# First unit's queries fetched and split inside the query stage of a cross-attention kernel, normalised rows spread over three pairs, last stores waited for later

## The reference, cut to what matters

```python
def _L0_xattn_ref(x, context, Wq, Wkv, Wo, ln_g, ln_b):   # x (16,64,256), context (16,1601,256)
    ctx = _layernorm(context, ln_g, ln_b)
    q = x @ Wq                                             # 16 heads of 64
    k, v = jnp.split(ctx @ Wkv, 2, axis=-1)
    ...
    sim = jnp.einsum('bhid,bhjd->bhij', q, k) * scale
    attn = jax.nn.softmax(sim, axis=-1)
    out = jnp.einsum('bhij,bhjd->bhid', attn, v)
    ...
x = x + _L0_xattn_ref(_layernorm(x), ctx_1024, ...)
```

## Time and profile before

| what | value |
|---|---|
| runs | 1813.75, 1817.82, 1817.73 us (median 1817.73) |
| profiled execution, its own time | 1818.62 us |
| its span in the trace | 1816.9 us |
| mean granted TensorE clock | 0.966 |
| PE busy | 1691.2 us, 93% of the span |
| DVE busy | 1469.1 us, 81% |
| ACT busy | 1233.8 us, 68% |

### The profile page before, as it was taken

How to read it: one execution, slowest core, us unless ns; L and a number is a source line. 1 busy time by engine, 2 the same in 40 slices (tenths; PEclk the granted TensorE clock), 3 DMA queues, 4 the chain that set the end, 5 groups by cost and what they waited for, 6 DMA issues and landing times. The chain is left out here.

```text
span 1816.9 us, 31835 instructions
## 1 busy us (share of the span) xinstructions
PE 1691.2 (93%) x9258; PEld 1391.5 (77%) x9258; DVE 1469.1 (81%) x2927; ACT 1233.8 (68%) x2224; POOL 129.7 (7%) x122
## 2 busy tenths in 40 slices
PE   6699999999999999999999999998889559999994
PEld 4478888888888888888888888886355349999994
DVE  5689999899989998999989998886346558788763
ACT  4567778778777777787777877866225247777751
POOL 0000000000000000000000000000012230000003
PEclk9899999999999999999999999999889779999996
DMA  7732222222313222222122222002850076666632
GB/s 268 284 89 60 85 78 69 72 78 62 88 56 89 68 78 69 79 64 88 55 86 69 82 70 84 26 24 71 275 183 27 26 243 221 194 230 216 197 103 75
DMA packets 172562, 199.01 MB, mean 110 GB/s; under 512 B 19129, under 2 KB 131921, under 8 KB 172497
## 3 DMA queue, kind: packets, MB, share of 16 engines
q1 hardware_dynamic: 170960, 194.00, 33.8%
q0 software_dynamic: 1536, 4.20, 0.7%
HBM read 153.53 MB, written 44.63 MB: 109 GB/s over the span
## 5 line engine op out<-in xcount | busy, mean ns | idle before, releaser
L757 ACT ACTIVATE s<-score,rnow 128x512 f32<-128x512 f32 (+1 forms) x416 | 286.4, 689 | 254.0 <-PE score L143 249.5
L141 PE MATMUL score<-qsh,tl 128*128 128x512 f32 (+1 forms) x832 | 331.3, 398 | 17.5 <-DVE qsl L816 15.2
L142 PE MATMUL score<-qsl,th 128*128 128x512 f32 (+1 forms) x832 | 325.6, 391 | 0.0
L141 PE MATMUL acc<-ph,cl 128*128 128x512 f32 (+1 forms) x832 | 324.8, 390 | 0.8 <-DVE pl L795 0.7
L143 PE MATMUL score<-qsh,th 128*128 128x512 f32 (+1 forms) x832 | 325.4, 391 | 0.0
L142 PE MATMUL acc<-pl,ch 128*128 128x512 f32 (+1 forms) x832 | 324.4, 390 | 0.0
L143 PE MATMUL acc<-ph,ch 128*128 128x512 f32 (+1 forms) x832 | 324.4, 390 | 0.0
L789 DVE TENSOR_TENSOR s<-s,misc 128x512 f32<-128x512 f32 (+1 forms) x416 | 281.7, 677 | 9.1 <-PE misc L720 7.6
L795 DVE TENSOR_TENSOR pl<-s,ph 128x512 fp32r<-128x512 f32 (+1 forms) x416 | 283.7, 682 | 1.6 <-ACT ph L738 1.6
L738 ACT ACTIVATE ph<-s 128x512 fp32r<-128x512 f32 (+1 forms) x416 | 258.9, 622 | 2.2 <-PE acc L143 1.7
L743 ACT ACTIVATE s<-s 128x512 f32<-128x512 f32 (+1 forms) x416 | 258.3, 621 | 2.1 <-DVE s L789 2.1
(11 more groups left out here) (249 smaller groups left out, 2768.1 us busy)
## 6 DMA issues: line engine op xcount, KB each, us to landing
raw<-in_ctx_in SPq DMA_DIRECT2D x192, 128.0 KB, 2.3
turned<-in_turned_in SPq DMA_DIRECT2D x48, 512.0 KB, 3.7
wr<-in_W SPq DMA_DIRECT2D x45, 512.0 KB
queries_scratch<-stage SPq DMA_DIRECT2D x32, 512.0 KB, 3.8
qr<-queries_scratch SPq DMA_DIRECT2D x64, 256.0 KB, 3.6
outputs_scratch<-o SPq DMA_DIRECT2D x64, 256.0 KB, 2.9
at<-outputs_scratch SPq DMA_DIRECT2D x16, 1024.0 KB, 7.5
wr<-in_Wg SPq DMA_DIRECT2D x15, 1024.0 KB
```

Source lines behind the costliest of these rows:

```text
L141: pe.matmul(out, wl, mh, start=first, stop=False, **more)
L142: pe.matmul(out, wh, ml, start=False, stop=False, **more)
L757: act.activation(s[0:n, u, t, :], score[0:n, slot(0, u, t) % 2, :], ACT.Copy, scale=rnow[0:n, t:t + 1]).then_inc(copied, 1)
```

## The change

Four edits. First, the raw and split buffers of the queries, their semaphores, and the semaphores of the stores move into an object `Queries` that lives through both stages; the first unit's load is issued in `queries` behind the stores of pair 4, and its splits stand in pair 5. Second, the 13 normalised rows are spread over pairs 5, 6 and 7. Third, the end of `queries` on SyncE waits for the stores of pairs 2 and 5 only (semaphore `stored[2]`); all stores are waited for before the load of the second unit (SyncE) and before the first copy of the second unit's scores (ScalarE). Fourth, GpSimd sets the columns first and clears afterwards.

```diff
+ROWS_BEHIND = {(5, 1): (0, 3), (6, 0): (3, 6), (6, 1): (6, 9), (7, 0): (9, 11), (7, 1): (11, KT)}
...
+class Queries:
+    def __init__(self, sb, sem):
+        self.raw = sb("qr", [P, DC, UQ], F32)
+        self.high = sb("qsh", [P, 2, DC, UQ], F32R)
+        self.low = sb("qsl", [P, 2, DC, UQ], F32R)
+        self.arrived, self.high_made, self.low_made = sem("q_in"), sem("qs_high"), sem("qs_low")
+        self.stored = [sem(f"stored{n}") for n in range(STAGES)]
+    def load(self, sp, QT, r, u):
+        for c in range(DC):
+            src = QT[u * PAIRS // 2:(u + 1) * PAIRS // 2, :, c, bass.ds(r, 1), :]
+            sp.dma_start(self.raw[:, c, :]..., src...).then_inc(self.arrived, 16)
+    def split_high(self, v, u, loads):
+        v.wait_ge(self.arrived, 16 * DC * loads)
+        v.tensor_copy(self.high[:, u], self.raw[:, :, :]).then_inc(self.high_made, 1)
+    def split_low(self, v, u, loads):
+        v.wait_ge(self.high_made, loads)
+        v.tensor_tensor(self.low[:, u], self.raw[:, :, :], self.high[:, u].bitcast(F32), ALU.subtract
+                        ).then_inc(self.low_made, 1)
... queries, SyncE
+                    if p == PAIRS // 2:
+                        for n, s in enumerate(stored):
+                            sp.wait_ge(s, 64 * len(range(n, PAIRS // 2, STAGES)))
+                        first.load(sp, QT, 0, 0)
                 sp.wait_ge(gb_in, 32)
-                for n, s in enumerate(stored):
-                    sp.wait_ge(s, 16 * 4 * len(range(n, PAIRS, STAGES)))
+                sp.wait_ge(stored[2], 64 * len(range(2, PAIRS, STAGES)))
... queries, VectorE, behind each take
+                        if (p, th) == (5, 0):
+                            first.split_high(v, 0, 1)
+                        if (p, th) == (5, 1):
+                            first.split_low(v, 0, 1)
+                            v.wait_ge(c_shift, 1)
+                        if (p, th) in ROWS_BEHIND:
+                            rows_normalised(*ROWS_BEHIND[p, th])
...
-                    if p >= 6:
-                        v.wait_ge(c_shift, 1)
-                        for t in range(7 * (p - 6), min(7 * (p - 5), KT)):
-                            ...
... attend, SyncE
-                    if (f := k.unit(-9)):
+                    if fetched(f := k.unit(-9)):
                         r, u = f
-                        wait(sp, q_low, unit(r, u))
-                        for c in range(DC):
-                            ...
+                        if begins(r) and u == 1:
+                            for i, landed in enumerate(stored):
+                                sp.wait_ge(landed, 64 * len(range(i, PAIRS, STAGES)))
+                        sp.wait_ge(q_low, unit(r, u))
+                        first.load(sp, QT, r, u)
... attend, GpSimd
-                clear(pool, earlier)
                 pool.memset(ch[:, :, 0:1].bitcast(F32), 1.0).then_inc(counting, 1)
                 pool.memset(cl[:, :, 0:1].bitcast(F32), 0.0).then_inc(counting, 1)
+                clear(pool, earlier)
... attend, ScalarE, before the copy of the scores
+                        if begins(r) and u == 1 and t == 0:
+                            for i, landed in enumerate(stored):
+                                act.wait_ge(landed, 64 * len(range(i, PAIRS, STAGES)))
... attend, VectorE: both splits now `if fetched(...)`, that is, not for the first unit
```

More of the change, by code:

```diff
@@ L224, in pool_root @@
         pool.tensor_tensor(self.shift[:, :], self.negmu[:, :], self.rstd[:, :], ALU.mult).then_inc(c_shift, 1)
+class Queries:
[8 more added lines that the diff above has]
+            src = QT[u * PAIRS // 2:(u + 1) * PAIRS // 2, :, c, bass.ds(r, 1), :]
+            sp.dma_start(self.raw[:, c, :].rearrange("p (k n) -> p k n", n=2 * NQ),
+                         src.rearrange("k p a n -> p k (a n)")).then_inc(self.arrived, 16)
+    def split_high(self, v, u, loads):
[5 more added lines that the diff above has]
+                        ).then_inc(self.low_made, 1)
 def queries(nc, res_x, x_in, ident, halfpow, Wq, WkT, QT, ctx_in, turned_in, turned_last, cx, gain, bias, ln_g, ln_b,
-            g_row, gb_in, turned0, spent):
+            g_row, gb_in, turned0, first, spent):
     with ExitStack() as ctx:
@@ L256, in queries @@
         k_made, k_act, k_dve = sem("k_made"), sem("k_act"), sem("k_dve")
-        stored = [sem(f"stored{n}") for n in range(STAGES)]
+        stored = first.stored
         raw_in, st_zero, st_made, c_mom, c_ve, c_rstd, c_shift = (
@@ L430, in low_queries, with rows_normalised @@
                                         ALU.subtract).then_inc(q_low, 1)
+                def rows_normalised(a, b):
+                    for t in range(a, b):
+                        m = rows(t)
+                        v.tensor_scalar(cx.nrm[0:m, t, :], cx.raw[0:m, t, :], cx.rstd[0:m, t:t + 1],
+                                        cx.shift[0:m, t:t + 1], ALU.mult, ALU.add).then_inc(normed, 1)
                 ln.vector_moments(v, x_in)
@@ L565, in inverse_rows, with attend @@
     return cx.nrm[:, PAIRS:PAIRS + 2, :].rearrange("p a b -> p (a b)")
-def attend(nc, ident, halfpow, ctx_in, turned_in, turned_last, cx, QT, OT, Wv, Wo, weights_in, turned0, earlier, spent):
+def attend(nc, ident, halfpow, ctx_in, turned_in, turned_last, cx, QT, OT, Wv, Wo, weights_in, turned0, first, earlier, spent):
     with ExitStack() as ctx:
@@ L582, in attend @@
         tl = sb("tl", [P, KT, DC, P], F32R)
-        qr = sb("qr", [P, DC, UQ], F32)
-        qh = sb("qsh", [P, 2, DC, UQ], F32R)
-        ql = sb("qsl", [P, 2, DC, UQ], F32R)
+        qh, ql = first.high, first.low
         s = sb("s", [P, 2, KT, UQ], F32)
@@ L599, in attend @@
         rated = sem("rated")
-        q_in = sem("q_in")
         o_out = [sem("o_out0"), sem("o_out1")]
@@ L604, in attend @@
         t_high, t_low, r_high, r_low = sem("t_high"), sem("t_low"), sem("r_high"), sem("r_low")
-        q_high, q_low = sem("qs_high"), sem("qs_low")
+        q_low, stored = first.low_made, first.stored
         scored, copied, maxed = sem("scored"), sem("copied"), sem("maxed")
@@ L621, in attend, with begins, fetched @@
         at_rows, at_rows_low = spread(LAG - KT + 1), spread(LAG - KT + 2)
+        def begins(r):
+            return isinstance(r, int) and r == 0
+        def fetched(f):
+            return f and not (begins(f[0]) and f[1] == 0)
         def later(found):
@@ L807, in step @@
                             v.tensor_tensor(top[0:n, :], top[0:n, :], s[0:n, u, t, :], ALU.max).then_inc(maxed, 1)
-                    if (f := k.unit(-5)):
+                    if fetched(f := k.unit(-5)):
                         r, u = f
-                        v.wait_ge(q_in, 16 * DC * (unit(r, u) + 1))
                         wait(v, scored, KT * (unit(r, u) - 1))
-                        v.tensor_copy(qh[:, u], qr[:, :, :]).then_inc(q_high, 1)
-                    if (f := k.unit(-4)):
+                        first.split_high(v, u, unit(r, u) + 1)
+                    if fetched(f := k.unit(-4)):
                         r, u = f
-                        v.wait_ge(q_high, unit(r, u) + 1)
-                        v.tensor_tensor(ql[:, u], qr[:, :, :], qh[:, u].bitcast(F32), ALU.subtract).then_inc(q_low, 1)
+                        first.split_low(v, u, unit(r, u) + 1)
                     for n, t in later(k.context(at_stats)):
```

11 lines of the change are left out of this document (3 added, 8 removed).

## The result

The changed kernel took 1807.68 us (median of 8 runs, 1803.22 to 1811.33) against 1817.84 us (8 runs, 1813.75 to 1823.42): ratio 0.9944, 95% interval 0.9928 to 0.9961, so 10.2 us less. Its profiled execution has a span of 1807.0 us, 9.9 less than the 1816.9 before.

A forecast was written before the change was run, and what follows sets the result against it. TensorE, busy all of 200 to 300 us, was taken as the bound, so an earlier start reaches the end whole. The terms -3.8 - 5.9 + 0.3 = -9.4 us gave 1808.3 us, range 1804.3 to 1812.6 us.

The forecast's parts named there:

- Term 1: Query stage's end: without SyncE's final wait for stores to land, the new block starts 3.8 us earlier.
- Term 2: New block's start: with queries already split and settings first, TensorE waits only for `tl`, starting 5.9 us earlier.
- Term 3: First units: raw tiles queue behind undrained stores, VectorE is late at `top`, costing TensorE 0.3 us.
- Counted from the end of the stores: Raw tile at the loop's start: stores end about 82.5 us, plus 2.0 to 3.9 us landing, gives 84.5 to 86.4.
- The text's own sign, 4 to 5 us from issue to landing: Sign for the new block's first tiles: raw to landing takes 4 to 5 us.
- without that cover each us would count: Query stage's end: the store queue hides VectorE delays up to 1.6 us; without it each us would cost.
- The sum: Whole kernel: -3.8 - 5.9 + 0.3 = -9.4 us, giving 1808.3 us, 0.52% faster.
- the span must follow within 1.5 us: Disproof sign: first score matmul near 80.7 us but span not following within 1.5 us means first units give it back.
- (a): Rival at the loop's start: raw tiles hold VectorE, costing 3 us instead of 0.3; 1811.0 us, chance 0.10.
- (c): Rival at the block's start: something else, such as SyncE's issues, holds it until stores land; 1812.1 us, chance 0.07.
- (d): Rival in the steady loop: it gets slower, at 0.8 us a pass 1820.3 us; chance 0.03.
- (b): Rival at the first score matmuls: TensorE's clock is still high at 80.7 us, saving 1.2 us; 1807.1 us, chance 0.09.

The follow-up runs named there:

- e5: Changed kernel with the last two of the query stage's 32 stores issued by ScalarE instead of SyncE; one run, 1805.94 us.
- e1: Changed kernel with GpSimd's 37 clears again ahead of its two column settings; one run, 1813.61 us.
- e10: e9 with the last two stores issued by ScalarE and 16 more matmuls behind TensorE's last query group; 1797.72 us (6 runs).
- e2: Changed kernel with SyncE waiting for all stores again at the query stage's end; one run, 1809.65 us.
- e4: Changed kernel with the normalised rows as before, seven behind pair 6 and six behind pair 7; one run, 1805.20 us.
- e6: Changed kernel with 16 further matmuls, result unused, behind TensorE's last group in the query stage; one run, 1806.85 us.
- e7: Changed kernel with the query weights' second, third and fourth parts split one pair earlier; 1805.40 us median of 4 runs.
- e9: e7 with the first unit's two query splits moved from pair 5 to pair 6; one run, 1799.91 us.
- e3: Changed kernel with the first unit's query load and both splits back in the attention block; one run, 1819.70 us.

## Why the prediction was right

**The gap and what stood behind it.** Predicted: from 15.20 to about 5 us, released by `tl`; measured 5.30, by `tl`. **Term 1**, 3.8 us: store to raw fell by 3.83 us, and SyncE's last issue was indeed next (e5 shows it by taking it away). **Term 2**, 5.9 us: raw to score fell by 5.84 us. GpSimd's part was put at 2.5 us and is 1.8 (e1, where 37 clears took 2.6 us; the 40 had taken 3.2). **Term 3**, 0.3 us, was zero: VectorE waited 1.57 us for the raw tile, its statistics began at 81.66 us, 3.1 us after TensorE's start, where 84.5 to 86.4 against 80.7 us (3.8 to 5.7) had been reckoned, and TensorE's wait for the last tile stayed 0.73 us. The step that failed is "Counted from the end of the stores": 2.0 to 3.9 us, the time from issue to landing, were added behind the end of the drain. The landing of SyncE's last store (issued at 75.83 us) says otherwise:

```profile
DMA to landing us min/median/max: 5.5/5.5/5.5
```

That store landed at 81.3 us, and the raw tile was there by 81.66: 0.3 us behind it and 4.15 us after its own issue at 77.51. The text's own sign, 4 to 5 us from issue to landing, was right and does not fit its 84.5 to 86.4 us. Where the block starts 1.8 us earlier against the store queue the term exists, at 0.2 us (e5), and with a fast start as well it is 0.6 us (e10).

**The query stage.** Predicted: the load lands at 66.0 to 67.2 us against 66.5 wanted, a wait of 0 to 0.7 us and no cost. In five traces there was a wait (0.4, 0.4, 0.5, 0.8 and 0.8 us in e2, e5, e1, e4 and e6), in the changed kernel's none. That none was luck: there the load had landed by 63.2 us and VectorE came for it at 64.30, after a stretch at the lower clock from 58 us on that cost the stage 1.5 us (last section); in the five others no such stretch lay between the load's issue and its use. The cover was there in all of them: the last store was issued 1.6 us after the last copy's end in the changed kernel, as predicted, and 1.2 to 1.5 us in e1, e2, e4 and e6. What the text called "without that cover each us would count" is e7: 2.97 us of wait in the same place, and it counts: with the splits a pair later (e9) the first score matmul comes 3.6 us earlier.

**What the two edits are worth apart.** The sum set 3.8 beside 5.9 as if each stood alone. Together they are, but the working never asked what one is worth without the other; e3 shows 0.48 us for the later wait alone.

**The absolute places** were off by 2 us: the first score matmul was expected near 80.7 us and came at 78.56. The part before the gap was 2.0 us shorter in that execution (last query matmul at 72.83 against 74.82 us); the last section shows 1.5 us of it as one stretch at the lower clock fewer. The span nevertheless followed by only 9.9 us, because the part behind the loop took 589.3 us instead of 587.5. By the text's own sign (the span must follow within 1.5 us) this would count against it; but the loop has the same length, so the first units gave nothing back, and the sign was drawn too narrow for the last part. In the twelve traces that part lies between 585.5 and 590.2 us without order, so a single time says nothing on 2 us here; the distances in the trace repeat to 0.01 us. One sum of the text is wrong: the forecast less 2.8 us is 1805.5, and its lower bound of 1804.3 us is the forecast less 1.2 for the clock and 2.8 for the spread.

**The rivals.** (a) did not come: the raw tile cost TensorE nothing. (c) fell: the block began 0.50 us after SyncE's last issue, 3.8 us before the last store landed. Its example was half right, since SyncE's long issues did hold the block, for 1.8 us (e5). (d) did not come: first to last score load is 1139.2 us against 1139.0. Of (b): the clock was at 0.73 over 78 to 79 us and at 0.50 over the next two,

(windows: length, busy us by engine, granted clock, DMA share, GB/s)

```profile
78.00:79.00 1.00, 0.45 (x1) 0.48 (x2) 1.00 (x4) 1.00 (x4) 0.00 (x0) 0.73 1.02 406
79.00:80.00 1.00, 1.00 (x4) 0.71 (x4) 1.00 (x4) 0.90 (x4) 0.00 (x0) 0.50 1.07 356
82.00:83.00 1.00, 1.00 (x6) 0.84 (x5) 1.00 (x4) 0.49 (x2) 0.00 (x0) 1.00 0.86 271
```

so it had just fallen when TensorE started. Less idle time would not have been enough: after 3.51 us of it (e5) 8 matmuls are slow, after 3.68 us (e7) 12. The prediction cited the Trainium skill (TensorE: Matmul & The Clock Gate, "The HAM clock gate") for the number of slow matmuls at a start differing from run to run. The traces agree as far as they go: 7 in the changed kernel and 12 in e4, with the same 1.05 us ahead of them and idle times of 5.30 and 5.46 us. No kernel here has two traces, so the same kernel against itself is not shown. It is a spread of 1 us that no edit here but e6's takes away.

## What to carry to other kernels

When a wait at a stage's end and a load at the next one's start are on one path, take both out: a load issued while the last stores still fill the queue lands behind them, and the wait reappears at its consumer. Ask of every transfer moved to an earlier place when it lands, not when it is issued, and ask again whenever the work around it becomes faster. Where a clock and a tail of the run move the time by more than the edit, read the edit off a distance between two instructions.

## What the runs showed of the hardware

The issue of a 512 KB store by SyncE took 0.33 us for the first stores of the stage and 1.15 us for the last, near one store's time on the DMA engines (512 KB at 406 GB/s, 1.3 us). Issued by ScalarE, the last two took 0.39 and 0.95 us in e5 and 0.40 and 0.34 us in e10, there with the DMA share at 1.01 (65 to 67 us). So full DMA engines alone do not stretch an issue; what else is needed, many transfers of the same issuer outstanding for one, is not shown.

A TensorE wait of 2.23 us for `wql` was followed by a granted clock of 0.50 for about 3 us in some places and not in others, with the same instructions on both sides. It fell after the first two of three such waits in the kernel before (0.53 over 30 to 32 us, 0.50 over 46 to 48), after the third alone in the changed one (0.50 over 58 to 60), after the second alone in e2. From one wait's end to the next it was 15.79 and 15.82 us before and 14.26 and 14.28 after: 1.5 us for each such stretch, as much as the slow start of the loop.

Two windows of the kernel before, one after its second wait and one after its third:

```profile
46.00:48.00 2.00, 2.00 (x6) 1.51 (x6) 0.69 (x1) 0.60 (x1) 0.00 (x0) 0.50 0.60 240
60.00:62.00 2.00, 1.77 (x8) 1.45 (x9) 1.90 (x11) 0.07 (x1) 0.00 (x0) 1.00 1.01 401
```

TensorE works through both (2.00 and 1.77 us busy), at a granted clock of 0.50 in the first and 1.00 in the second.
